# Adjacency attention with layernorm on one core: A's products regrouped, its first tiles first, and Wv split during the first scores

## The reference

```python
q = jnp.einsum('bnd,ed->bne', x, Wq)
k = jnp.einsum('bnd,ed->bne', x, Wk)
v = jnp.einsum('bnd,ed->bne', x, Wv)
rel = jnp.einsum('bnd,bmd->bnm', q, k)
rel = adjacency.T[None, :, :] * rel
rel = rel / jnp.linalg.norm(rel, axis=2, keepdims=True)
out = layernorm(x + jnp.einsum('bnm,bmd->bnd', rel, v))
```

## Time and profile before

| | us |
|---|---|
| median of 3 runs | 1971.78 (1971.39 to 1971.95) |
| the profiled execution | 1971.97 |
| its span, first to last instruction | 1970.2 |
| TensorE busy | 1957.0 (99%) |
| VectorE, ScalarE, GpSimd busy | 1531.9, 762.5, 957.8 |
| TensorE's idle stretches in the launch, sum of the five that are listed as waits | 7.2 |
| TensorE starts A / Y / S / V of batch 0 | 6.00 / 19.21 / 46.24 / 85.21 |

### The profile page before, as it was taken

The page is one execution under the profiler, slowest core; times in us unless marked ns, Lnnn a source line. Parts: engine busy times, 40 slices in busy tenths (PEclk is TensorE's granted clock), DMA queues, the critical chain, the costliest instruction groups (busy, mean ns, idle before and its releaser), DMA issues.

```text
span 1970.2 us, 28685 instructions
## 1 busy us (share of the span) xinstructions
PE 1957.0 (99%) x9857; PEld 1669.1 (85%) x9857; DVE 1531.9 (78%) x2085; ACT 762.5 (39%) x1288; POOL 957.8 (49%) x639
## 2 busy tenths in 40 slices
PE   8999999999999999999999999999999999999998
PEld 6888888888888888888888888888888888888887
DVE  8796877868778696787968779687796877868775
ACT  5433434335342352423424234342433424335341
POOL 5744536455354553446435374453644536455352
PEclk9999999999999999999999999999999999999999
DMA  5734343344524345343444333443434343344401
GB/s 188 314 134 165 144 167 115 144 154 154 186 92 149 142 157 184 122 151 118 157 175 160 128 139 133 172 153 128 160 128 170 144 155 127 144 154 152 185 26 64
DMA packets 80416, 292.22 MB, mean 148 GB/s; under 512 B 7441, under 2 KB 7441, under 8 KB 76305
## 3 DMA queue, kind: packets, MB, share of 16 engines
q1 hardware_dynamic: 80400, 292.06, 40.2%
HBM read 251.13 MB, written 40.89 MB: 148 GB/s over the span
## 4 chain that ended last, share of the span: by engine, by line
PE 97%; DVE 1%; POOL 1%; DMA 0%; issue 0%; SPq 0%; ACT 0%; POOLq 0%; DVEq 0%
PE banks L422 32%; PE banks L424 32%; PE banks L423 32%; DMA scr<-xT 0%; DVE aw L794 0%; DVE x_lo L755 0%; POOL scr L1063 0%; DVE yv L816 0%; POOL square_sum L1067 0%; POOL squares L1067 0%; SPq L344 0%; POOL scr L1072 0%; SPq L343 0%; POOL res L1075 0%; POOL res L1080 0%
## 5 line engine op out<-in xcount | busy, mean ns | idle before, releaser
L422 PE MATMUL banks<-yv 128*128 128x512 f32 x1024 | 399.8, 390 | 0.0
L424 PE MATMUL banks<-yv 128*128 128x512 f32 x1024 | 398.5, 389 | 0.0
L423 PE MATMUL banks<-yv 128*128 128x512 f32 x1024 | 398.5, 389 | 0.0
L1119 POOL TENSOR_TENSOR square_sum<-square_sum,squares 128x512 f32<-128x512 f32 x224 | 319.9, 1428 | 85.7 <-ACT squares L657 75.1
L422 PE MATMUL banks<-yv,x_hi 128*128 128x512 f32 x896 | 348.7, 389 | 0.5 <-DVE rel L857 0.5
L424 PE MATMUL banks<-yv,x_lo 128*128 128x512 f32 x896 | 348.6, 389 | 0.0
L423 PE MATMUL banks<-yv,x_hi 128*128 128x512 f32 x896 | 348.6, 389 | 0.0
L1136 POOL TENSOR_TENSOR rstd<-var_eps,minus_half 128x1 f32<-128x1 f32 x128 | 144.2, 1127 | 329.3 <-DVE var_eps L968 329.3
L423 PE MATMUL banks<-aw,x_hi 128*128 128x256 f32 x896 | 253.6, 283 | 0.0
L424 PE MATMUL banks<-aw,x_lo 128*128 128x256 f32 x896 | 253.5, 283 | 0.0
L422 PE MATMUL banks<-aw,x_hi 128*128 128x256 f32 x896 | 253.5, 283 | 0.0
(11 more groups left out here) (108 smaller groups left out, 3430.5 us busy)
## 6 DMA issues: line engine op xcount, KB each, us to landing
scr<-adj SPq DMA_DIRECT2D x128, 512.0 KB, 5.8
aw<-w_kept SPq DMA_DIRECT2D x16, 3584.0 KB, 11.1
aw<-a_kept SPq DMA_DIRECT2D x15, 3584.0 KB, 11.0
scr<-xT SPq DMA_DIRECT2D x32, 1024.0 KB, 7.1
res<-x SPq DMA_DIRECT2D x128, 256.0 KB, 2.7
out<-res SPq DMA_DIRECT2D x128, 256.0 KB, 2.0
a_kept<-aw SPq DMA_DIRECT2D x1, 3584.0 KB, 18.2
w_kept<-v_raw SPq DMA_DIRECT2D x3, 512.0 KB, 8.5
```

Source lines behind the costliest of these rows:

```text
L422: pe.matmul(bank_ap, l_hi, r_hi, start=first and i == 0, stop=False, skip_group_check=on)
L423: pe.matmul(bank_ap, l_hi, r_lo, start=False, stop=False, skip_group_check=on)
L424: mm = pe.matmul(bank_ap, l_lo, r_hi, start=False, stop=i == len(pairs) - 1, skip_group_check=on)
L1119: pool.tensor_tensor(square_sum[:, h, :], square_sum[:, h, :], squares[:, n % SQRING, :], ALU.add).then_inc(square_added, 1)
```

## The change

TensorE's products of A are regrouped: in each slice first those of two high parts, then those of Wq's rests, then those of Wk's rests, with a semaphore wait ahead of each kind; and the four banks are done two by two in the last two slices. The fill products are gone. Of x, the half with rows 0 to 511 is loaded and split first. The first sums S1 and S2 move from VectorE to GpSimd and go to places of their own, and A's T3 is split on GpSimd. Wv leaves the beginning: its sums and low parts move from GpSimd to VectorE, into the first pair of scores of batch 0, its high parts on ScalarE behind the first two squares, and both are written straight into `aw`. So batch 0 has no load of `w_kept`; the seven stores of it become one, issued when the seventh low part is made. In every batch the pieces X11, X22 and S2, S3 change places.

```diff
-X_PIECES = (X22, X11, S1, X12, S3, S2, S4)
-X_SUMS = (S1, S3, S2, S4)
+X_PIECES = (X11, X22, S1, X12, S2, S3, S4)
+X_SUMS = (S1, S2, S3, S4)
...
                 if first:
-                    for i in range(3, 7):
-                        store_wv(i)
-                    load_adj(2)
-                    sp.wait_ge(a_split, 7)
+                    sp.wait_ge(a_split, len(A_PIECES))
+                    sp.wait_ge(a_t3_split, 1)
                     sp.dma_start(a_kept, aw[:, :].bitcast(F32)).then_inc(a_stored, DMA)
+
+                    sp.wait_ge(w_loaded, DMA)
+                    sp.dma_start(w_kept, aw[:, :].bitcast(F32)).then_inc(w_stored, DMA)
                     for t in range(RRING):
                         load_res(0, t)
...
+            for ks, js in (((0, 1), range(KD)), ((2, 3), (0, 1)), ((2, 3), (2, 3))):
+                for k in ks:
+                    pe.wait_ge(w_hi_made, 2 * k + 2)
+                    for j in js:
+                        pe.matmul(bank[A_BANK + j], wq_hi[:, k, cols(j)], wk_hi[:, k, :], start=(k == 0), stop=False,
+                                  skip_group_check=True)
+                    pe.wait_ge(w_split, 2 * k + 1)
+                    for j in js:
+                        pe.matmul(bank[A_BANK + j], wq_lo[:, k, cols(j)], wk_hi[:, k, :], start=False, stop=False,
+                                  skip_group_check=True)
+                    pe.wait_ge(w_split, 2 * k + 2)
+                    for j in js:
+                        mm = pe.matmul(bank[A_BANK + j], wq_hi[:, k, cols(j)], wk_lo[:, k, :], start=False,
+                                       stop=(k == KD - 1), skip_group_check=True)
+                        if k == KD - 1:
+                            mm.then_inc(a_done, 1)
...
-            for i in range(FILL_PRODUCTS):
-                pe.matmul(bank[0], zeros[:, 0:P], zeros[:, 0:BANK], start=True, stop=True)
...
+                act.wait_ge(a_stored, DMA)
+                act.wait_ge(y_done, Y_COUNT)
+                act.activation(wv_hi[:, q, :, :], wv_raw_of[q], ACT.Copy).then_inc(wv_hi_made, 1)
...
+            def wv_lo_piece(i):
+                q = WV_PIECES[i]
+                dve.wait_ge(wv_hi_made, i + 1)
+                lo = dve.tensor_tensor(wv_lo[:, q, :, :], wv_raw_of[q], wv_hi[:, q, :, :].bitcast(F32), ALU.subtract)
+                if i == 6:
+
+                    lo.then_inc(w_loaded, DMA)
...
+                if first and pair == 0:
+                    for q in WV_SUMS:
+                        wv_sum_of(q)
                 if pair == 0:
                     for j in range(2):
                         y_lo_piece(b, B22, j, y_b22_raw[j])
...
+            pool.wait_ge(x_loaded[1], DMA)
+            pool.tensor_tensor(first_raw_of[S1], x21_raw, raw_of[X22], ALU.add).then_inc(first_sum[S1], 1)
             pool.wait_ge(first_sum[S1], 1)
-            pool.wait_ge(x_loaded[0], DMA)
-            pool.wait_ge(a_split, 1)
+            pool.wait_ge(x_split, x_place[S1])
+            pool.tensor_tensor(first_raw_of[S2], first_raw_of[S1], raw_of[X11],
+                               ALU.subtract).then_inc(first_sum[S2], 1)
+            pool.wait_ge(a_hi_made, a_hi_place[T3])
+            pool.tensor_tensor(a_lo[:, T3, :, :], a_raw_of[T3], a_hi[:, T3, :, :].bitcast(F32),
+                               ALU.subtract).then_inc(a_t3_split, 1)
+            pool.wait_ge(x_split, x_place[S2])
             pool.tensor_tensor(raw_of[S3], raw_of[X11], x21_raw, ALU.subtract).then_inc(first_sum[S3], 1)
             pool.wait_ge(first_sum[S2], 1)
-            pool.wait_ge(x_split, x_place[X12])
-            pool.tensor_tensor(raw_of[S4], raw_of[X12], raw_of[S2], ALU.subtract).then_inc(first_sum[S4], 1)
```

More of the change, by code:

```diff
@@ L97, in adjacency_attention_layernorm @@
         a_stored = sem("a_stored")
-        w_stored = [sem(f"w_stored{i}") for i in range(WSLOTS)]
+        w_stored = sem("w_stored")
         a_loaded = sem("a_loaded")
@@ L594, in a_hi_piece @@
                 act.activation(a_hi[:, q, :, :], a_raw_of[q], ACT.Copy).then_inc(a_hi_made, 1)
-            for q in (X22, X11, S1):
-                x_piece(0, q, True)
+            x_piece(0, X11, True)
             a_hi_piece(B11)
             act.activation(a12_raw, a_block(0, 1), ACT.Copy).then_inc(a12_copied, 1)
-            for q in (B21, B22, T1):
+            x_piece(0, X22, True)
+            a_hi_piece(T1)
+            x_piece(0, S1, True)
+            x_piece(0, X12, True)
+            for q in (B21, B22):
                 a_hi_piece(q)
-            x_piece(0, X12, True)
-            a_hi_piece(T2)
             def y_hi_piece(b, q, j, source):
@@ L828, in y_blocks @@
                 a, bb, c = y_bank["a"], y_bank["b"], y_bank["c"]
-                for j in range(2):
-                    y_lo_piece(b, B11, j, a[j])
-                if first:
-                    dve.wait_ge(a_split, 7)
+                if not first:
+                    for j in range(2):
+                        y_lo_piece(b, B11, j, a[j])
                 for j in range(2):
@@ L839, in y_blocks @@
                 if first:
-                    x_piece(0, S4)
+                    x_piece(b, S3, True)
+                    for j in range(2):
+                        y_lo_piece(b, B11, j, a[j])
+                    x_piece(b, S4, True)
+                    a_lo_piece(B22)
+                    dve.wait_ge(a_split, len(A_PIECES))
+                    dve.wait_ge(a_t3_split, 1)
                 for j in range(2):
@@ L887, in s_blocks @@
                     dve.tensor_tensor(c22(i), bb[i % 2], c22(i), ALU.add).then_inc(s_c22, 1)
+                if first and pair == 0:
+                    wv_lo_piece(0)
+                    wv_lo_piece(1)
                 for i in tiles:
@@ L891, in s_blocks @@
                     dve.tensor_tensor(c21(i), c[i % 2], c21(i), ALU.add).then_inc(s_c21, 1)
+                if first and pair == 0:
+                    wv_lo_piece(2)
+                    wv_lo_piece(3)
                 for i in tiles:
@@ L900, in s_blocks @@
                     dve.tensor_tensor(c12(i), bb[i % 2], c12(i), ALU.add).then_inc(s_c12, 1)
+                if first and pair == 0:
+                    for n in (4, 5, 6):
+                        wv_lo_piece(n)
                 for i in tiles:
@@ L1018, in _ @@
             y_first(0)
-            for q in (T4, T3):
-                a_lo_piece(q)
-            a_lo_piece(B22)
+            a_sum_of(T4)
+            a_lo_piece(T4)
             batch(0, True, False)
@@ L1080, in _ @@
[L1080 to L1082 removed]
+            pool.tensor_tensor(raw_of[S4], raw_of[X12], first_raw_of[S2], ALU.subtract).then_inc(first_sum[S4], 1)
             def t1_raw(b, j):
```

150 lines of the change are left out of this document (61 added, 89 removed).

## The result

| | median (range, runs), us | profiled execution | its span |
|---|---|---|---|
| kernel before | 1971.74 (1971.39 to 1972.30, 6) | 1971.97 | 1970.2 |
| changed kernel | 1979.53 (1978.90 to 1980.46, 6) | 1978.9 | 1977.1 |

The ratio of the times is 1.0040, with a 95% interval of 1.0027 to 1.0053. The time forecast was 1978.8, in a range of 1971.5 to 1981.5.

A forecast was written before the change was run, and what follows sets the result against it. TensorE, busy 99% of the span, was taken to bound the kernel. A gain of 1.1 us by V's start, then losses of 5.3, 0.4 and 2.4 (clock), made +7.0 on 1971.78: 1978.8, range 1971.5 to 1981.5.

The forecast's parts named there:

- What bounds the kernel: Whole launch: TensorE is busy 99% of the span; its five waits make 7.2 us, all in the first 50 us.
- Part 1: A at the start: runs from 5.1 to 16.2, Y begins directly behind it, 3.0 us gained.
- Part 2: Y: waits of 1.3, 1.8 and 2.4 us, clock stays up, S begins at 41.2, 5.0 us gained so far.
- Part 3: First scores: VectorE's turns with GpSimd make TensorE wait 3.5 and 1.0 us; V starts at 84.1, 1.1 gain left.
- the 1.0 for the next pair's `s_u2`: First scores: TensorE wants `s_u2` of the next pair at 72.1, VectorE has it at 73.1, a 1.0 us wait.
- Part 4: V's third round: store ahead of adjacency tiles puts tile 6 at 85.9; TensorE waits 5.2 us; sum so far +4.6.
- The 0.4 at the outputs: Where the outputs begin in batch 0: a last TensorE wait of 0.4 us for V's low parts.
- Part 5: V, behind the 5.2 us wait: the granted clock falls, costing 2.9 us less the outputs' share, +2.4.
- the clock stays: V: no clock fall behind the long wait, everything else as forecast, 1976.4 us; chance 0.25.
- The tiles are not late: V: transfers don't queue behind the store, or it lands within 6 us; 1971 to 1974 us, chance 0.16.
- VectorE is not held: First scores: a VectorE turn costs 0.6 us, not 1.7, so the 5.0 gain stands; 1966.8 us, chance 0.08.
- As slow as A's store: Store ahead of the tiles takes 18.2 us instead of 10.5, slowing V by 7 more; 1986 us, chance 0.06.

The follow-up runs named there:

- the halved store: Changed kernel with the store of `w_kept` in two halves, high parts ahead of adjacency tiles 6 and 7, low parts behind them: 1973.96 us, ratio 1.0012.
- the program written out: Changed kernel with batch 0 of TensorE's program written out ahead of the loop and nothing else: 1979.34 us.
- the late store: Changed kernel with the store of `w_kept` and four loads of x issued behind adjacency tiles 6 and 7: 1971.49 us, ratio 0.9999.

## Why the prediction came true, point by point

The sum, the sign and the place of every large wait were right, and the forecast is 0.7 us from the median. Its terms were not all right; some errors cancelled.

- **What bounds the kernel.** The five waits of the list are read with one slip: one of the "three shorter ones" is 1.3 long, longer than the 0.7 ahead of A. It stands ahead of the idle products in both kernels, and nothing hangs on it.
- **Part 1.** A was to run from 5.1 to 16.2; it ran from 5.64 to 16.65, the weights having come later in this execution (ScalarE's first high part at 4.44 for 3.99). Y follows directly, as the step said.
- **Part 2.** Two of three waits hit: 1.8 forecast and 1.76 measured for T2, 2.4 and 2.03 for T4. The first, 1.3 for S1, fell short: TensorE stood 0.2 us there, since x and S1 were 0.7 earlier than assumed and A 0.45 later. The clock stayed up, as the step let it; but that was chance, since behind the same two waits it fell in five of eight other profiled executions. S was to begin at 41.2 and began at 40.42: 5.8 gained and not 5.0.
- **Part 3.** The step carries the scores fully: turns of 1.7 (1.65 to 1.78), `s_r` the one that is late, a wait of 3.5 (3.54). Two things behind it were wrong and cancelled. I let the clock stay after this wait; it fell, 1.6 us. And the 1.0 for the next pair's `s_u2` was not there, because TensorE came later itself. It did come (1.2) with the halved store and with the program written out, whose clock stayed up in the scores. So the net price of the fall is 0.1 to 0.2: from TensorE's restart behind `s_r` to V it is 26.21 here and 26.06 in those two. V began at 83.98 for 84.1: with VectorE's `s_r` setting the pace, errors ahead of it (0.8 at S's start) don't show. `s_r` itself let TensorE go on at 57.8 and not 58.4, and the extra time behind it was 0.5 more than forecast: that these cancel is luck.
- **Part 4.** The mechanism is the one forecast, and the late store shows it alone (8.0 us). Tile 6 at 85.9 was exact, out of two small errors: the store was issued at 70.96 and not 71.3, and took 11.0 to land and not 10.5. The term mis-sized is the chain behind it: I took 8.4 from tile 6 to ScalarE's copy, as before, which holds only if tile 7 follows closely. It followed 2.9 later, the chain took 9.9 (9.0 where tile 7 came 1.4 behind, GpSimd's two masks taking 3.4 there and 2.56 in the earlier trace rows), and the wait was 6.5 and not 5.2. The 0.4 at the outputs did not appear in the changed kernel; with the clock held up in V it was there as 0.6 (a wait for `yv`).
- **Part 5.** The clock fell behind V's wait, as forecast, here and in all three other profiled executions with a wait of 5.9 to 6.6. It held for 14 matmuls of 256 columns and so cost 1.3; I had priced it as in Y, 2.9 less 0.4. From V's start on it is 8.2 measured (28.50 from V to the load of A, 20.34 before) and 8.1 forecast. That these agree is luck: the wait was 1.3 longer, the clock cost 1.1 less than its term of 2.4, and the 0.4 at the outputs was not there. Keeping TensorE busy in V was worth 1.0 to 1.2 in the medians; in the kernel written out the clock cost 2.2 there, and with it held up 0.6 came back as a wait for V's low parts.

The rivals: "the clock stays" falls by the granted clock; its price, measured by keeping TensorE busy, is 1.0 to 1.2 and not 2.4. "The tiles are not late" and "VectorE is not held" fall by the rows of after. "As slow as A's store" falls too: 14.9 from the issue to tile 6, with 1.5 MB of loads behind the 3.5 MB of store.

The Trainium skill (TensorE: Matmul & The Clock Gate, Part 1) has the chip judge activity in windows that run freely and don't begin with the kernel's work. The runs fit this: behind one and the same wait of about 2 us in Y the clock falls in one execution and stays in another. So the rule bears on parts 2 and 3, where I took the clock's staying as given.

## What to carry to other kernels

An ordered DMA queue is part of the critical path: before a large transfer is put on it, ask which small one behind it somebody needs, and when. Work that is moved to another engine can cost more there than where it was, if the new engine takes turns with the old one: price it by the rows in which the two engines run side by side. And time that TensorE saves, or loses, ahead of a wait for another engine's chain vanishes in that wait: price the last wait of a stage first, and a loss ahead of it at nothing as long as it is shorter than that wait.

## What the runs showed of the hardware that I had not expected

- SP's issues can themselves be held up behind a large store: four of 256 KB took 4.00 us directly behind the 3.5 MB of `w_kept`, and the two of 512 KB behind them 2.54, where two took 0.93 with no store ahead of them. Behind half the store it was 4.07 and 0.99. It is not the size alone: in the kernel before, four of 256 KB took 2.21 directly behind A's store of 3.5 MB (49.11). What sets it stays open.
- The granted clock falls behind short waits too, and not each time. Behind a pair of waits in Y of 1.7 to 1.9 and 1.85 to 2.15 it fell in five profiled executions and stayed in four. Behind waits of 3.5 to 6.6 it fell in all nine cases. In the scores of the changed kernel it was still full when TensorE restarted at 57.77 and fell 0.8 later (0.65 in the stretch from 58 to 60).
- What a fall costs is not one figure: 1.3 us in V of the changed kernel and about 2.2 at the same place in the one written out, 1.6 in the scores, and in Y 1.6 behind about 2 us of wait and 2.9 behind 4.2. In V the granted clock went down at about 92.8 in the changed kernel and at 95.0 in the one written out, with TensorE's restart at 96.42 and 96.55: more of the low stretch fell into the wait in the first.
- Two tiles issued together were usable 1.4 us apart in two profiled executions and 2.4 to 2.9 apart in four.
- The beginning is not equally long each time: in eleven profiled executions with the same code for A, Y began between 16.40 and 17.56. The latest (the late store) has A's first four products from 5.63 to 7.55, the changed kernel from 5.64 to 6.67. The profile gives the full clock for both stretches, and the cause stays open. Differences under 1 us between single executions are therefore no evidence here; the medians are.
